# Two transformer layers on one core: q and k as two fp16 parts with scales made on the chip, heads in partition halves

## What is computed

```python
q = split_heads(layernorm(x) @ Wq + bq)          # layer 1: no biases, weights transposed
k = split_heads(layernorm(x) @ Wk + bk)
attn = einsum('bhqd,bhkd->bhqk', q, k) / sqrt(16)
attn = attn + slopes[h] * (arange(T) - (T - 1))   # layer 0 only
attn = where(causal, attn, -big)
p = softmax(attn);  o = p @ v;  x = x + o @ Wo (+ bo)
```

## Time and profile before

| what | value |
|---|---|
| runs (median, lowest, highest) | 438.63, 436.85, 438.97 us |
| profiled execution, first to last instruction (the only time known of it) | 441.7 us |
| PE busy | 410.0 us, 93% |
| DVE busy | 297.1 us, 67% |
| ACT busy | 232.9 us, 53% |
| POOL busy | 170.2 us, 39% |
| mean granted clock of PE | 0.980 |
| DMA | 22.97 MB, of which 19.03 MB on SP's and ACT's queue q1 |

### The profile page before, as it was taken

How to read it: one execution, slowest core, us unless ns; L and a number is a source line. 1 busy time by engine, 2 the same in 40 slices (tenths; PEclk the granted TensorE clock), 3 DMA queues, 4 the chain that set the end, 5 groups by cost and what they waited for, 6 DMA issues and landing times.

```text
span 441.7 us, 14528 instructions
## 1 busy us (share of the span) xinstructions
PE 410.0 (93%) x6328; PEld 237.2 (54%) x6328; DVE 297.1 (67%) x596; ACT 232.9 (53%) x377; POOL 170.2 (39%) x250
## 2 busy tenths in 40 slices
PE   5799789999999988999999998998999999888997
PEld 5356564555555347544377466544555553465476
DVE  4636489999998216521336586899999981188883
ACT  3535355577776973221101541655877769635950
POOL 4107013314033144478692000234361544453770
PEclk9989799999999999999999997999999999999999
DMA  6899550000000000200100479400000000000002
GB/s 204 129 239 263 128 148 4 4 3 4 4 2 5 4 1 6 65 8 9 64 0 0 120 200 224 106 5 4 3 4 3 4 5 2 2 1 0 1 26 71
DMA packets 21657, 22.97 MB, mean 52 GB/s; under 512 B 2588, under 2 KB 20858, under 8 KB 21594
## 3 DMA queue, kind: packets, MB, share of 16 engines
q1 hardware_dynamic: 20498, 19.03, 17.8%
q0 software_dynamic: 544, 2.49, 1.9%
q10 hardware_dynamic: 552, 0.53, 0.4%
HBM read 8.27 MB, written 1.05 MB: 21 GB/s over the span
## 4 chain that ended last, share of the span: by engine, by line
PE 71%; DVE 14%; ACT 4%; DMA 3%; issue 3%; POOL 2%; SPq 2%; ACTq 0%; DVEq 0%
PE ps L785 11%; PE ps L765 11%; DVE mx L1258 11%; PE ps L743 10%; PE ps L916 8%; PE ps L1012 5%; PE ps L944 4%; PE ps L921 4%; ACT prob L1141 4%; PE ps L677 4%; PE ps L980 4%; DMA col_rows<-in_L_ffn_up_scale 3%; PE ps L845 3%; PE ps L751 2%; POOL xn L605 1%
## 5 line engine op out<-in xcount | busy, mean ns | idle before, releaser
L1258 DVE TENSOR_REDUCE mx<-ps 128x1 f32<-128x512 f32 (+3 forms) x304 | 181.1, 654 | 28.9 <-PE ps L751 24.1
L1141 ACT ACTIVATE prob<-ps 128x1024 f32<-128x1024 f32 (+1 forms) x192 | 145.4, 812 | 63.4 <-PE ps L765 63.1
L743 PE MATMUL ps<-kS,qS 96*32 96x512 bf16 (+21 forms) x1536 | 111.9, 321 | 4.4 <-DVE mx L1258 3.0
L590 POOL TENSOR_SCALAR_AFFINE_SELECT prob<-prob 128x256 f32<-128x256 f32 x128 | 51.9, 412 | 163.9 <-ACT prob L1141 162.5
L765 PE MATMUL ps<-qS,kS 101*32 101x512 bf16 (+7 forms) x1536 | 95.2, 326 | 3.7 <-ACT prob L1141 3.6
L785 PE MATMUL ps<-prob,v 128*32 128x512 f32 (+3 forms) x768 | 80.1, 489 | 0.6 <-POOL prob L590 0.4
L743 PEld LDWEIGHTS ps<-kS,qS 99*32 99x32 bf16 (+1 forms) x1536 | 42.8, 95 | 50.4 <-DVE mx L1258 28.1
L748 PE MATMUL ps<-mask_q,identb 128*32 128x32 bf16 (+1 forms) x1024 | 51.1, 186 | 2.7 <-issue 2.7
L765 PEld LDWEIGHTS ps<-qS,kS 101*32 101x32 bf16 (+1 forms) x1536 | 35.0, 96 | 31.2 <-ACT prob L1141 15.8
L751 PE MATMUL ps<-mask_q,identb 128*32 128x64 bf16 (+1 forms) x512 | 45.4, 198 | 0.0
L748 PEld LDWEIGHTS ps<-mask_q,identb 128*32 128x32 bf16 x1024 | 28.1, 98 | 14.0 <-issue 9.2
(11 more groups left out here) (146 smaller groups left out, 537.0 us busy)
## 6 DMA issues: line engine op xcount, KB each, us to landing
qS<-parts SPq DMA_DIRECT2D x24, 128.0 KB, 3.3
kS<-parts SPq DMA_DIRECT2D x24, 128.0 KB, 3.4
qS<-prob SPq DMA_DIRECT2D x12, 128.0 KB, 8.0
kS<-prob SPq DMA_DIRECT2D x12, 128.0 KB, 7.5
qS<-xn SPq DMA_DIRECT2D x12, 128.0 KB, 3.4
kS<-xn SPq DMA_DIRECT2D x12, 128.0 KB, 2.9
out<-x SPq DMA_DIRECT2D x8, 128.0 KB, 1.7
oT<-in_L_ffn_gate_w POOLq DMA_DIRECT2D x1, 768.0 KB, 4.8
```

The lines of the kernel that those rows point to most:

```text
L590: nc.gpsimd.affine_select(out=square, in_=square, compare_op=ALU.is_ge, fill=0.0, base=0, pattern=[[0, 2], [1, P]], channel_multiplier=-1) ...
L743: mmi = nc.tensor.matmul(span[r:r + STRIP, 0:seen], qS[0:K_MAX[L], c, g * G + h, qt * P + r:qt * P + r + STRIP], kS[0:K_MAX[L], g * G + h, ...
L1141: nc.scalar.activation(prob[:, n % 3, 2 * pair:2 * pair + 2, off:CH], ps[:, 2 * (m % 2):2 * (m % 2) + 2, off:CH], ACT.Exp, scale=SCALE).th ...
L1258: ins = nc.vector.tensor_reduce(mx[:, slot, qt, heads[0]:heads[-1] + 1, part], src, AX_X, ALU.max)
```

## The change

q and k become two fp16 parts each (hi and lo), and their product a sum over three pairs: 48 rows for a head. fp16 has a narrow range, so q and k are first multiplied by powers of two. These come from bounds on the norm of each projection: DVE takes statistics of Wq and Wk (`square_weights`), PE sums the squares over the partitions (`norms`), ACT copies the sums out, POOL raises them to the power -0.5 (`invert_norm`), and DVE makes the scales and their inverse (`scales`). The exponential's scale is now a number for each partition in SBUF (`exp_scale`) instead of a constant in the instruction. The rows for the position bias in `qS` are made on the chip (`scale_row`).

With its extra rows a head has at most 53 rows. Even heads now stand in partitions 0 to 63 and odd ones in 64 to 127 (`place`). The channel order becomes (head pair, mt, d), so that a q/k job holds the eight even or the eight odd heads; the first piece of the attention therefore waits for jobs 0 to 3 instead of 0 and 1, and the fourth for all eight. Score and mask matmuls have 64 or fewer rows in one half; v's matmuls still have 128.

An item of the maxima now holds at most two heads of one parity: the item with four heads of 128 keys becomes two items of 256 columns, so there are 160 items in a layer and not 152. The maxima's DMA becomes two, one for each half. The parts' tiles move to a tile of their own (`hidden`), which layer 0's hidden values and later the third weight of layer 1's feed-forward also use; so ACT waits for that weight's rounding (`w8_round`, 3) ahead of layer 1's feed-forward.

```diff
-Q_PARTS = (0, 0, 0, 1, 1, 2)
-K_PARTS = (2, 0, 1, 0, 1, 0)
+Q_PARTS = (0, 0, 1)
+K_PARTS = (0, 1, 0)
+def place(h):
+    return h % 2 * HALF, h // 2
...
-        per = CH // keys
-        items += [(qt, 1, tuple(range(h, h + per)), CH * c, keys) for h in range(0, G, per)]
+        if keys <= CH // 2:
+            items += [(qt, 1, (h, h + 2), CH * c, keys) for h in range(2)]
+        else:
+            items += [(qt, 1, (h,), CH * c, keys) for h in range(G)]
...
             def spread(L, k):
-                for part, done in enumerate((hi_done, mid_done, lo_done)):
+                for part, done in enumerate((hi_done, lo_done)):
...
             def spread_max(L, cg):
-                sp.dma_start(qS[K_MAX[L]:K_EXP[L], c, g * G:(g + 1) * G, :], mT[:, cg % 2, :]).then_inc(m_stacked[cg % 2], 16)
+                for m in range(2):
+                    rows = slice(m * HALF + K_MAX[L], m * HALF + K_EXP[L])
+                    sp.dma_start(qS[rows, c, g * G // 2:(g + 1) * G // 2, :], mT[m * G * TPC:(m + 1) * G * TPC, cg % 2, :]).then_inc(m_stacked[cg % 2], 16)
...
             rstd_of(0)
+            invert_norm(0)
             rstd_of(1)
...
             def exp_scores(L, s, pair):
+                    base, slot = place(h)
+                    rows, half = slice(base, base + K_EXP[L]), slice(base, base + HALF)
                     for r in range(0, P, STRIP):
-                        mmi = nc.tensor.matmul(bank[r:r + STRIP, off:CH], kS[0:K_EXP[L], h, kt * P + r:kt * P + r + STRIP],
-                                               qS[0:K_EXP[L], c, h, off:CH], start=True, stop=not masked)
+                        mmi = nc.tensor.matmul(bank[r:r + STRIP, off:CH], kS[rows, slot, kt * P + r:kt * P + r + STRIP],
+                                               qS[rows, c, slot, off:CH], start=True, stop=not masked)
...
+                if L == 0:
+                    norms(0)
...
-                        nc.scalar.activation(part_slots[n][:, 0], ps[:, 4 + job % 4], ACT.Identity, bias=bias).then_inc(hi_done, 1)
-                    if n >= 1 and n != QK_FIRST:
-                        middle(n - 1)
+                    if n == 0:
+                        act.wait_ge(scale_done, L + 1)
+                    nc.scalar.activation(part_slots[n][:, 0], ps[:, 4 + job % 4], ACT.Identity, bias=bias,
+                                         scale=qk_scale[:, L, w:w + 1]).then_inc(hi_done, 1)
...
-                                             ps[:, 2 * (m % 2):2 * (m % 2) + 2, off:CH], ACT.Exp, scale=SCALE).then_inc(s_free, 1)
+                                             ps[:, 2 * (m % 2):2 * (m % 2) + 2, off:CH], ACT.Exp, scale=exp_scale[:, L:L + 1]).then_inc(s_free, 1)
...
+            def square_weights(L):
+                for m in range(2):
+                    if L == 0:
+                        dve.wait_ge(w0_in[m], 16)
+                    for j in range(CJ):
+                        chain(nc.vector.bn_stats(w_stats[:, m * CJ + j], w[:, m, j]))
...
                 if tiles.stop == TPC:
                     ln_normalise(0, 0)
+                    square_weights(0)
```

More of the change, by code:

```diff
@@ L284, in alibi_tail @@
 def alibi_tail():
-    bf16 = mybir.dt.np(BF16)
+    half = mybir.dt.np(FP16)
     start = 2.0 ** -0.5
@@ L292, in alibi_tail @@
     for _ in range(3):
-        part = rest.astype(bf16)
+        part = rest.astype(half)
         rows.append(part)
         rest = rest - part.astype(np.float32)
-    rows += [np.ones((NH, T), bf16)] * (MAX_ROWS + ALIBI_ROWS[0])
-    apart = np.zeros((len(rows), NH * NC, CH + TAIL_GAP), bf16)
-    apart[:, :, 0:CH] = np.stack(rows).reshape(len(rows), NH * NC, CH)
-    return apart
+    rows += [np.full((NH, T), MAX_UNIT, half)] * MAX_ROWS
+    apart = np.zeros((len(rows), 2, N_SLOT * NC, CH + TAIL_GAP), half)
+    apart[:, :, :, 0:CH] = np.stack(rows).reshape(len(rows), N_SLOT, 2, NC, CH).transpose(0, 2, 1, 3, 4).reshape(len(rows), 2, N_SLOT * NC, CH)
+    return apart.view(mybir.dt.np(BF16))
 def two_layer_kernel(nc, a, out, tail):
@@ L361, in two_layer_kernel @@
         w8m = oT[:, :, :].rearrange("p g t -> p (g t)")[:, CJ * HID1:2 * CJ * HID1]
-        w8_down = [parts[:, 2 * n:2 * n + 2].rearrange("p n r q -> p (n r q)").bitcast(F32) for n in range(2)]
+        w8_down = [words[:, n * HT * C:(n + 1) * HT * C] for n in range(2)]
         gu1 = sb("gu1", [P, 2, CJ, HID1], FP16)
@@ L518, in _ @@
                     sp.wait_ge(pv_done, N_STEP)
-                    sp.dma_start(k_chunks[K_MAX[1]:K_EXP[1]], tail[ALIBI_ROWS[0]:ALIBI_ROWS[0] + MAX_ROWS, :, 0:CH]).then_inc(ones_k, 16)
+                    for m in range(2):
+                        rows = slice(m * HALF + K_MAX[1], m * HALF + K_EXP[1])
+                        sp.dma_start(k_chunks[rows], tail[ALIBI_ROWS[0]:, m, :, 0:CH]).then_inc(ones_k, 16)
             yout = out.rearrange("o (t p) c -> p (o t) c", p=P)
@@ L643, in _ @@
                 round_columns(w8, w8m, dst, slice(0, CJ * HID1)).then_inc(w8_round, 1)
+            invert_norm(1)
             rstd_of(4)
             rstd_of(5)
-            for n in range(4):
+            for n in range(6):
                 pool.wait_ge(stacked[n], 16 * len(Q_PARTS) * 2)
@@ L740, in max_scores @@
                     span = bank[:, i * keys:(i + 1) * keys]
+                    base, slot = place(g * G + h)
+                    rows, half = slice(base, base + K_MAX[L]), slice(base, base + HALF)
+                    one = identb[half, base:base + STRIP]
                     for r in range(0, P, STRIP):
                         seen = keys if part == 0 or r == P - 2 * STRIP else keys - P + r + STRIP
-                        mmi = nc.tensor.matmul(span[r:r + STRIP, 0:seen], qS[0:K_MAX[L], c, g * G + h, qt * P + r:qt * P + r + STRIP],
-                                               kS[0:K_MAX[L], g * G + h, key0:key0 + seen], start=True, stop=part == 0)
+                        mmi = nc.tensor.matmul(span[r:r + STRIP, 0:seen], qS[rows, c, slot, qt * P + r:qt * P + r + STRIP],
+                                               kS[rows, slot, key0:key0 + seen], start=True, stop=part == 0)
                     if part == 1:
@@ L982, in products_down1, with norms @@
                     mmi.then_inc(b_full, 1)
+            def norms(L):
+                bank = take_a(("norm", L))
+                pe.wait_ge(w_squared, L + 1)
+                terms = [(unit[:, 0:1], w_sq[:, L, :, j]) for j in range(CJ)]
+                if L == 0:
+                    terms += [(unit[:, 1:2], b_sq[:, :, j]) for j in range(CJ)]
+                for n, (one, rhs) in enumerate(terms):
+                    mmi = nc.tensor.matmul(bank[:, 0:2], one.to_broadcast([P, P]), rhs, start=n == 0, stop=n == len(terms) - 1)
+                mmi.then_inc(a_full, 1)
             def turn_bqk():
@@ L1053, in qk_parts @@
             def qk_parts(L):
-                def middle(m):
-                    act.wait_ge(b_free, B_AT["qk", L, m] + 1)
-                    nc.scalar.copy(part_slots[m][:, 1], rest[:, m % 2]).then_inc(mid_done, 1)
-                for n in range(N_QK + 1):
+                for n in range(N_QK):
                     if n == QK_FIRST:
-                        middle(n - 1)
                         drain_transposed("xnT", L, range(TPC, NT))
```

236 lines of the change are left out of this document (158 added, 78 removed).

## The result

The changed kernel takes 457.31 us (median of 4 runs, 455.35 to 465.06), the kernel before 437.99 in the same comparison (436.85 to 438.97): a ratio of 1.042, 95% interval 1.038 to 1.046. The ratio is taken without the run of 465.06 us, whose clock was lower than that of the others (0.919, for 0.944 to 0.959). The forecast was 433. The profiled execution took 456.3 us and spans 454.6, for 441.7 before. Its mean granted clock of TensorE is 0.947, for 0.980.

The account below looks back on a forecast made before the run. PE and DVE were taken as both full in the attentions' middles, other losses at layer 0's start. Terms 2.5+4.0+1.5+0.5+0.5-2.6-0.6-0.3 give 5.5 us off the 441.7 span: 436.2, so median 433; range 421 to 446.

Parts of the forecast that it names:

- The middles: Middle stretches of both attentions: half the rows relieve PE despite changes of row mode, winning 1.25 us each, 2.5 in all.
- Rival D: Slower: changes of row mode cost 0.42 us a step, PE becomes the only bound in both attentions, 444 us; chance 0.21.
- The gap of 0.1 to 0.2 us on each side of a v product: Sign in PE's timeline that would show the forecast's changes between 64-row and 128-row matmuls.
- The 1.25: Gain in us taken for each attention's middle stretch, out of between 4.2 and a loss.
- The stop and half clock at 47 us: Layer 0's start: halving the q/k DMAs removes PE's 2.7 us stop and half clock behind it, +4.0 us (bounds 0, 5.7).
- the 3.1 us: How far the profiled execution's 441.7 us span was put above the median of 438.63; taken off 436.2 to give 433.1.
- The scale chain: Layer 0's start: scale work delays the first hi part 2.6 us, PE's scale-vector wait may shorten: +1.5; ACT's wait, separately, +0.5.
- Layer 1's start: Start of layer 1's attention: side jobs run at half clock, which stays; between -1 and +1.9 us, taken as +0.5.
- The exponentials: Scale in SBUF makes each exponential 0.09 us longer, showing only behind the last maxima: -1.3 us a layer, -2.6 in all.
- The last transpose: End of each attention: no v product covers DVE's work before the last transpose, -0.3 us a layer, -0.6 in all.
- The rest: Layer 1's statistics and scales lie in layer 0's feed-forward, where DVE idles; PE's sums cost -0.3 us.
- The second maxima DMA: Attentions: its issue on SP could delay PE, 8.7 us if all 14 transits counted fully; taken inside the middles' 1.25.

Follow-up runs that it names:

- e5: Changed kernel plus two idle matmuls of 128 rows and 128 columns ahead of every maxima item of the first four pieces: 479.78 us.
- e6: Changed kernel plus the same number of idle matmuls at the same places, but with 32 rows and 32 columns: 545.08 us.
- e7: Kernel before the change, its score matmuls reading 48 rows fewer, all heads still at partition 0: 674.56 us.
- e3: Changed kernel with the DMAs of layer 0's feed-forward weights behind those of the fourth q/k job instead of the second's: 458.79 us.
- e16: Changed kernel in which VectorE takes the maximum over only the first half of the keys for items off the diagonal: 450.66 us, one run.
- e12: Kernel before the change plus one idle matmul of 64 rows and 32 columns at each step of the exponentials: 452.75 us, ratio 1.029.
- e17: Kernel before the change in which VectorE takes the maximum over only the first half of the keys for items off the diagonal: 433.13 us, one run.
- e8: e3 plus layer 1's weights behind the first maxima's DMA and the idle matmuls of e5: 487.63 us.
- e9: Changed kernel, new SyncE order: feed-forward and layer 1 weights behind the fourth job, then the first maxima's DMA, then jobs 4 to 7: 457.62 us.
- e13: Changed kernel with the new SyncE order of e9 in layer 0 alone: 457.36 us.
- e15: Kernel before the change, DMAs of jobs 4 and 5 behind the first maxima's, 6 and 7 behind the second's: 436.61 us for 438.12, ratio 0.997.
- e10: Changed kernel plus four idle 128-row matmuls only behind a v product, and at every second item before a layer's first: 461.41 us.
- e11: Changed kernel with e9's order, e10's idle matmuls and the exponential's scale as a number in the instruction: 460.47 us.

## Why the prediction was wrong

*The middles (+2.5).* This is the step that failed. It weighed TensorE's rows only as time: half the rows save, the ways in and out cost, VectorE caps the gain. It took the clock of 1.00 there for granted. Both attentions together now have 37.6 us of half clock behind their first copies, for 8.2, and the first four distances lost 6.0 and 1.9 us; e5, e6 and e7 show that a smaller share of the array in use is enough for such falls. Where the two can be told apart, most of the loss is clock, not all of it: in e3 the third and fourth distance of layer 0 ran at the full clock and took 16.9 and 17.9 us, for 19.3 and 19.5 in the changed kernel and 16.6 and 17.4 before. So of the 4.8 us that these two lost, 4.0 go with the clock. Rival D named the right side and the wrong reason: 0.42 us a step was guessed, 0.24 is measured, less than what the halves save, and the fifth and sixth distance lose nothing. The gap of 0.1 to 0.2 us on each side of a v product, which the forecast named as a sign, is there.

*The gain of the rows at the full clock.* The 1.25 was wrong: it is 0.0 in the late pieces. VectorE's idle time of 4 us in 80 is not TensorE's to give back; it is there with TensorE 94% busy as with 100%. Nor is VectorE shown to be the floor: e16 took over 3 us off it, and a piece fell by 0.4. The halves do run at once: a pair holds 0.24 us, for 0.44 before.

```profile
114.86 0.41 PE L818 MATMUL ps<-qS,kS 53*32 53x512 f16 x8
115.10 0.39 PE L794 MATMUL ps<-kS,qS 51*32 51x512 f16 x4
```

By the page TensorEngine Tiling (Array Packing) of the Trainium skill, section Overview, that is the up to 2x of two small tiles, and here it is 1.8. At the full clock it was worth nothing.

*The stop and half clock at 47 us (+4.0).* It goes with the traffic, as I took it: it comes in four executions whose queues were full up to it (before, e3, e12, e17) and in none where they were nearly empty (e8, e9, e13, e15). In before an instruction DMA of 16 KB starts within 0.2 us of it, at 47.0. Full queues are not enough, though: e7 has a DMA share of 1.13 from 44 to 45 us and such a DMA at 44.1, and no stop, so what stops the engine is not shown. But I read SyncE's new order, put it into the text, and did not ask what job 3 stands behind, now that the first piece waits for it: that is the new stop of 6.5 us, and 1.06 in e3 with the weights behind it. The price was probably wrong too: it came from a profiled execution that spans 441.7 us, where 34 others of the same kernel have a median span of 437.1, and e15, which takes the stop out, is only 1.5 us faster. I went from the span of that one execution to the median of all and kept the full stop as a gain, so I may have counted part of it twice. And the 3.1 us compare a span with a time: in all 34 the time is 1.7 us above the span, so the profiled one lies 4.8 us above the median.

*The scale chain (+1.5).* The first hi part comes at 16.9 us for 13.3, 3.6 later, not 2.6. TensorE's wait for the scale vectors is gone, and so is its 0.82 us wait for ScalarE. With the order mended (e9, e13) the first copy comes 4.7 and 4.6 us earlier than before the change, of the 6.0 forecast for these three terms.

*Layer 1's start (+0.5).* The way to the first copy costs 0.9, and the next distance is 3.9 shorter: 3.0 won. The two side jobs of the earlier trace rows now stand ahead of that copy, at the full clock:

```profile
276.23 2.00 PE L725 MATMUL ps<-w1T,xnT 128*128 128x256 f32 x8
```

Taken without this gain, the second to fourth distance of layer 1 lose 5.8 us, nearly the 6.0 of layer 0's four.

*The exponentials (-2.6)* cost 88 ns each, as forecast, and 1.1 us in layer 0's last distance and tail (e10 against e11), for 1.3 a layer. *The last transpose (-0.6)*: 11 exponentials instead of 10 start in the last distance, it grows by 1.2, and the tail does not shrink: in layer 0 the two together lose 1.3 for both terms, forecast 1.6 a layer. *The rest*: 56.7 us for 56.6. *The second maxima DMA* does not show: TensorE waits 0.4 us in all for the maxima's DMAs, its weight loads 0.7.

## What to carry to other kernels

Matmuls with fewer rows do not only free TensorE: they leave more of its array unused, and this can cost the clock of the whole stretch (0.50 for 1.00 here), so ask of each change that thins the matmuls what the engine does per microsecond afterwards. When a piece of work gets a new dependency, read the whole queue ahead of what it now waits for. A loss read from one profiled execution is worth only what the other executions have of it.

## What was not expected of the hardware

- Score matmuls with 51 instead of 99 rows (e7) ran both attentions at 1.2 GHz with TensorE busy throughout: the span is 678.3 us for 441.7, the mean clock 0.657 for 0.980.
- Two idle matmuls ahead of each item, 0.30 us together at the full clock, kept the clock at 1.00 with 128 rows and columns; with 32 rows and columns it stayed at 0.50, with TensorE busy for 73.29 of 73.3 us.
- A way into the 64-row form and back cost 0.24 us around the v products of the changed kernel and 0.16, an idle matmul included, in e12, both with stationary operands of 32 columns, where the nearest row of before gave 0.31.
